# Side work of a three-part recurrent loop cut into small pieces and spread over its steps

## The reference, cut to what matters

```python
def lstm(prev_h, prev_c, xz_t):                 # L2 cond
    i, f, o, g = gates(xz_t + prev_h @ Wh)
    next_c = f * prev_c + i * g
    return o * tanh(next_c)

xp = silu(h @ W_in.T)                           # L2 attn, h from the LSTM
k, v, q, beta = ...                             # projections of xp, beta by a sigmoid
def step(S, inp):
    kn = k / (norm(k) + 1e-06)
    delta = v - einsum('bhij,bhj->bhi', S, kn)
    S = tanh(beta[..., None] * S + delta[..., None] * kn[..., None, :])
    Sq = einsum('bhij,bhj->bhi', S, q)
    return S, Sq * silu(Sq)
x = x + cell_out @ W_out.T

next_h = tanh(prev_h @ Wh + x_t @ Wx)           # L2 cond2, on the new x
```

## Time and profile before

| what | us |
|---|---|
| median of 3 runs | 3451.38 |
| lowest and highest | 3448.74, 3456.43 |
| the profiled execution | 3455.16 |
| its span, first to last instruction | 3453.4 |

### The profile page before, as it was taken

The page is one execution under the profiler, slowest core; times in us unless marked ns, Lnnn a source line. Parts: engine busy times, 40 slices in busy tenths (PEclk is TensorE's granted clock), DMA queues, the critical chain, the costliest instruction groups (busy, mean ns, idle before and its releaser), DMA issues. The chain is left out here.

```text
span 3453.4 us, 94785 instructions
## 1 busy us (share of the span) xinstructions
PE 2884.6 (84%) x35913; PEld 2169.6 (63%) x35915; DVE 1844.7 (53%) x7113; ACT 1151.5 (33%) x4428; POOL 761.3 (22%) x1477
## 2 busy tenths in 40 slices
PE   5889999956888894688899998987447799999988
PEld 3557888843556664456666666665314478888755
...
GB/s 75 2 2 0 0 0 0 0 33 1 2 2 0 1 0 64 96 76 65 87 85 64 86 87 63 79 95 59 37 0 1 2 0 0 0 0 0 0 0 12
DMA packets 106860, 101.37 MB, mean 29 GB/s; under 512 B 95616, under 2 KB 95616, under 8 KB 97536
## 3 DMA queue, kind: packets, MB, share of 16 engines
...
## 5 line engine op out<-in xcount | busy, mean ns | idle before, releaser
L578 POOL TENSOR_TENSOR l2r_beta_s<-l2r_state,l2r_beta_f 128x256 f32<-128x256 f32 x512 | 366.7, 737 | 547.0 <-ACT l2r_state L484 477.9
L484 ACT ACTIVATE l2r_state<-l2r_pre 128x256 f32<-128x256 f32 x512 | 190.5, 416 | 255.4 <-DVE l2r_pre L707 255.4
L381 PE MATMUL l2r_o_ps<-l2r_rows,l2r_outer 32*128 32x128 f32 x2048 | 207.0, 492 | 49.4 <-DVE l2r_rows L699 49.4
L707 DVE TENSOR_TENSOR l2r_pre<-l2r_o_ps,l2r_beta_s 128x256 f32<-128x256 f32 x512 | 193.5, 419 | 67.3 <-PE l2r_o_ps L381 66.2
L369 PE MATMUL l2r_d_ps<-l2r_state,l2r_kq 128*32 128x128 f32 x2056 | 206.3, 419 | 14.9 <-ACT l2r_state L484 13.4
L381 PEld LDWEIGHTS l2r_o_ps<-l2r_rows,l2r_outer 32*128 32x128 f32 x2048 | 139.2, 306 | 77.5 <-issue 70.5
L347 PEld LDWEIGHTS l2r_r_ps<-l2r_r_ring,main_even_layers 128*128 128x128 f32 x512 | 128.9, 312 | 92.4 <-issue 80.2
L699 DVE TENSOR_TENSOR l2r_rows<-l2r_d_ps,main_even_layers 128x128 f32<-128x128 f32 x257 | 74.5, 290 | 172.8 <-PE l2r_d_ps L369 162.0
L334 PEld LDWEIGHTS l2r_lstm_ps<-l2r_h_ring,l2r_w_part 128*128 128x128 bf16 x3072 | 103.5, 105 | 93.3 <-DVE l2r_h_low L693 53.7
L347 PE MATMUL l2r_r_ps<-l2r_r_ring,main_even_layers 128*128 128x8 f32 x512 | 149.3, 365 | 9.6 <-ACT l2r_r_ring L492 9.6
L133 PE MATMUL l3r_acc<-l3r_xw,main_base 128*128 x512 | 154.9, 389 | 1.6 <-issue 1.6
...
## 6 DMA issues: line engine op xcount, KB each, us to landing
l2r_beta_f<-l2r_beta_store SPq DMA_DIRECT2D x256, 256.0 KB, 7.0
...
l2r_beta_store<-l2r_beta_tok SPq DMA_DIRECT2D x256, 8.0 KB, 1.5
...
l2r_v_store<-l2r_v_part SPq DMA_DIRECT2D x128, 24.0 KB, 2.0
...
```

The source lines that it names most:

```text
L381: last = nc.tensor.matmul(o_ps[:, c, 0:P], outer[chunk_rows(c), n // TC % 2, n % TC, :, :].rearrange("p a b -> p (a b)"), rows[chunk_rows( ...
L484: nc.scalar.activation(state[:, h * 2 * P:(h + 1) * 2 * P], pre[:, h * 2 * P:(h + 1) * 2 * P], ACT.Tanh).then_inc(state_ready[h], 1)
L578: nc.gpsimd.tensor_tensor(beta_s[:, half], state[:, half], beta_f[:, q % BETA_SLOTS, n % QUARTER, half], ALU.mult).then_inc(s["bs_ready"], 1)
L707: nc.vector.tensor_tensor(pre[:, half].rearrange("p (c n) -> p c n", c=2), o_ps[:, 2 * h:2 * h + 2, 0:P], beta_s[:, half].rearrange("p (c ...
```

## The change

The LSTM's bank becomes two (`lstm_psa`, `lstm_psb`), each with the sums of eight LSTM steps and eight RNN steps; the inputs are written in halves, one gate of eight steps (64 columns) at a time, at steps given by `LSTM_PIECES`, and the RNN's inputs in three pieces of one, eight and seven steps. The token projections become six 128-column products at steps 2 to 7, q one product at each of steps 9 and 10, the transposes go to step 11. The square root becomes a guess by a shift and three Newton iterations, 14 operations of 128x8 on POOL at steps 6 to 8; DVE waits for them at step 8. The product for kn_tok goes from DVE to POOL, step 9; the squares go from POOL to ACT, step 10; POOL's k layouts are two each at steps 13 and 14. Stores of kn, v and beta are 2, 2 and 4 DMAs a wave; beta is stored first and v is loaded ahead of beta. In DRAM the step now lies inside the batch, so beta_f arrives in runs of 512 B (4 steps x 32 values) where a partition's run was 8,192 B. The amount of data is the same.

```diff
-        v_store = nc.dram_tensor(f"{tag}_v_store", (3 * HEADS2, 2, TC, BH, N2), BF16, kind="Internal").ap()
-        beta_store = nc.dram_tensor(f"{tag}_beta_store", (4, TC, 2, 2, BH, N2), F32, kind="Internal").ap()
+        v_store = nc.dram_tensor(f"{tag}_v_store", (3 * HEADS2, 2, BH, TC, N2), BF16, kind="Internal").ap()
+        beta_store = nc.dram_tensor(f"{tag}_beta_store", (4, 2, HG, BH, TC, N2), F32, kind="Internal").ap()
...
+        def lstm_at(n, first, last):
+            at = n % TCH * 4 * B
+            return lstm_ps[n % TC // TCH][:, at + first * B:at + last * B]
+        def rnn_at(n, count=1):
+            half, slot = (1, n % TC - 1) if 1 <= n % TC <= TCH else (0, (n - TCH - 1) % TC)
+            at = (4 * TCH + slot) * B
+            return lstm_ps[half][:, at:at + count * B]
...
+        LSTM_PIECES = {0: (0,), 3: (1,), 4: (2,), 5: (3,)}, {1: (0, 1), 2: (2,), 4: (3,)}
...
+                def rnn_inputs(w, lo, hi):
+                    if lo == 0:
+                        pe.wait_ge(s["x_added"], w + 1)
+                        pe.wait_ge(s["r_ready"], w * TC + 1)
+                    if lo == 1:
+                        pe.wait_ge(s["h_ready"], min((w + 4) * TC, T) + 1)
...
-                    if step in (2, 3):
+                    if 2 <= step < 8:
...
+                        if what >= 1:
+                            pe.wait_ge(s["kv_ready"], 2 * w + what)
+                        cols = HEADS2 * N2 // 2
+                        to, of = (what % 2 * 2 + part) * cols, (what * 2 + part) * cols
+                        last = nc.tensor.matmul(m_ps[:, to:to + cols], xp[:, :], w_tok[:, of:of + cols], start=True, stop=True)
+                        if part == 1:
+                            last.then_inc(s[("k_psum", "v_psum", "beta_psum")[what]], 1)
+                    if step in (9, 10):
+                        g = step - 9
+                        pe.wait_ge(s["beta_in"], w + 1)
+                        last = nc.tensor.matmul(m_ps[:, (2 + g) * CH:(3 + g) * CH], w_q[:, g * P:(g + 1) * P], xp[:, :],
+                                                start=True, stop=True)
+                        if g == 1:
+                            last.then_inc(s["q_psum"], 1)
...
-                        if rnn is not None and step >= 1:
+                        if rnn is not None:
+                            if step == 0:
+                                rnn_inputs(rnn, 0, 1)
                             rnn_product(rnn * TC + step)
                         if delta is not None:
                             spread_delta(n)
+                        if lstm is not None:
+                            if rnn is not None and step in (0, TCH):
+                                pe.wait_ge(s["r_ready"], rnn * TC + step + 2)
+                            lstm_products(lstm * TC + step)
+                        if step % TCH == 0 and has_bias(k, int(step == 0)):
+                            lstm_bias(*((k, 1) if step == 0 else (k + 1, 0)))
                         if rnn is not None and step == 0:
-                            rnn_inputs(rnn)
-                            rnn_product(rnn * TC)
+                            rnn_inputs(rnn, 1, TCH + 1)
+                        if rnn is not None and step == TCH:
+                            rnn_inputs(rnn, TCH + 1, TC)
                         if lstm is not None:
-                            if lstm >= 1 and step == 0:
-                                lstm_bias(lstm)
-                                for g in range(4):
-                                    lstm_inputs(lstm, g)
-                            lstm_products(lstm * TC + step)
+                            lstm_pieces(lstm, step, rnn)
...
-                    if step == 6:
-                        act.wait_ge(s["ssq_ready"], w + 1)
-                        nc.scalar.activation(norm[:, :], ssq[:, :], ACT.Sqrt).then_inc(s["norm_ready"], 1)
...
+                    if step >= 13:
+                        for g in ((0,), (1, 2), (3,))[step - 13]:
...
+                        nc.scalar.activation(sq_sq[:, :, :], sq[:, :, :], ACT.Square).then_inc(s["sq_sq_ready"], 1)
...
+                    pool.wait_ge(s["root_ready"], 14 * w + 4 * k + part + 2)
+                    if part == 0:
+                        last = nc.gpsimd.tensor_tensor(norm[:, :], ssq[:, :], root, ALU.mult)
+                    if part == 1:
+                        last = nc.gpsimd.tensor_tensor(norm[:, :], norm[:, :], root, ALU.mult)
+                    if part == 2:
+                        last = nc.gpsimd.tensor_scalar(norm[:, :], norm[:, :], -0.5, 1.5, ALU.mult, ALU.add)
+                    if part == 3:
+                        last = nc.gpsimd.tensor_tensor(root, root, norm[:, :], ALU.mult)
+                    last.then_inc(s["root_ready"], 1)
...
+                        pool.wait_ge(s["root_ready"], 14 * w + 1)
+                        nc.gpsimd.tensor_scalar(guess[:, :], guess[:, :], -1, 0x5F375A86, ALU.mult,
+                                                ALU.add).then_inc(s["root_ready"], 1)
+                        for part in range(4):
+                            root_part(w, 0, part)
+                    if step == 7:
+                        for part in range(4):
...
+                    if step == 9:
+                        pool.wait_ge(s["inv_ready"], 2 * (w + 1))
...
+                        nc.gpsimd.tensor_tensor(kn_tok[:, :, :], k_tok[:, :, :],
+                                                inv[:, :].unsqueeze(2).broadcast_to([P, HEADS2, N2]), ALU.mult).then_inc(s["kn_ready"], 1)
...
-                    if step in (12, 13, 14, 15):
+                    if step in (13, 14):
                         pool.wait_ge(s["knt_ready"], w + 1)
-                        g, h = divmod(step - 12, 2)
...
-                    if step == 2:
+                    if step == 1:
...
+                        dve.wait_ge(s["ssq_ready"], w + 1)
+                        nc.vector.tensor_scalar(guess[:, :], ssq[:, :].bitcast(I32), 1, None,
+                                                ALU.logical_shift_right).then_inc(s["root_ready"], 1)
+                    if step == 8:
...
+                        dve.wait_ge(s["beta_psum"], w + 1)
+                        if w >= 1:
+                            dve.wait_ge(s["beta_stored"], 16 * 4 * w)
+                        nc.vector.tensor_tensor(beta_tok[:, :], m_ps[:, 0:HEADS2 * N2], beta_bias, ALU.add).then_inc(s["beta_in"], 1)
...
-                        dve.wait_ge(s["inv_ready"], 2 * w + 2)
...
-                        nc.vector.tensor_tensor(kn_tok[:, :, :], k_tok[:, :, :],
-                                                inv[:, :].unsqueeze(2).broadcast_to([P, HEADS2, N2]), ALU.mult).then_inc(s["kn_ready"], 1)
...
-                    if step == 11:
...
-                    if step == 12:
...
+                        sp.dma_start(beta_f[chunk_rows(m), q % BETA_SLOTS, :, :, :].rearrange("p c t i -> p c (t i)"),
+                                     beta_store[m, :, :, :, part * QUARTER:(part + 1) * QUARTER, :].rearrange("h g b t i -> (h g b) (t i)")
+                                     .unsqueeze(0).broadcast_to([32, 2 * HG * BH, QUARTER * N2])).then_inc(beta_loaded[q % BETA_SLOTS], 16)
...
+                    for h in range(2):
                         for g in range(HG):
-                            sp.dma_start(beta_store.rearrange("m t h g b i -> g h b t m i")[g, h, n],
-                                         beta_tok[TC * b:TC * (b + 1), g * P:(g + 1) * P].rearrange("p (m i) -> p m i", i=N2)
+                            sp.dma_start(beta_store[:, h, g].rearrange("m b t i -> (b t) m i"),
+                                         beta_tok[BH * TC * h:BH * TC * (h + 1), g * P:(g + 1) * P].rearrange("p (m i) -> p m i", i=N2)
...
                     if proj is not None:
+                        store_beta(proj)
                         store_kn(proj)
                         load_kn(proj)
                         store_v(proj)
-                        store_beta(proj)
+                        load_v(proj)
                         load_beta(proj, 0)
-                        load_v(proj)
```

220 lines of the change are left out of this document (107 added, 113 removed).

## The result

The changed kernel takes **3345.9 us** (median of 4 runs, 3342.7 to 3348.9); the kernel before 3453.1 us (4 runs, 3448.7 to 3456.4). The ratio is 0.969, with a 95% interval of 0.9673 to 0.9707: 107 us or 3.1% less. 3351 us was forecast, with a range of 3325 to 3398. The profiled execution has a span of 3340.9 us beside 3453.4 before, 112.5 less.

The account below looks back on a forecast made before the run. PE was taken as nearly full, steps bound by the delta chain or PE's work. Gains of 68 (waves), 12 (start), 13 (waves 0 and 1) and 8 (last steps), less 0.5, made 100.5 us: 3351 us, range 3325 to 3398.

Parts of the forecast that it names:

- The step law: Layer 2 loop: a step lasts the larger of the 3.25 us delta-state chain and PE's 2.64 us plus side work.
- The 0.5 us for handovers: Added to the 59.2 us wave for handovers between engines that the packed picture leaves out, giving 59.7 us.
- the 1 us added to waves 0 and 1: Handover allowance on the first two waves, forecast at 55.4 and 58.4 us; their gain was put at 13 us.
- The cut pieces: PE side work: some 14 halved products a wave, 64 columns each, priced at 0.50 us apiece.
- the rival with the lone price: Each cut piece on PE costs the 0.73 us of a product standing alone; 3391 us, chance 0.08.
- the lower bound: A 64-column piece on PE costs only its share of the columns, 0.24 us, giving a wave of 56.5 us.
- Both waits: From step 15 to 0, PE's 3.03 us wait for v and POOL's 4.13 us for beta go, 4 us in hand.
- the one-step RNN input: PE side work from step 15 to 0, priced at 0.35 us beside the output pair; period 4.03 us.
- The root: Steps 6 to 8: 14 POOL operations at 0.28 us finish at 8.6 us, before DVE at 10.4 us, so hidden.
- The table loads: ACT loses three loads of 1,283 ns a wave, blocked 3.9 us; gain already inside the 65.4 us wave.
- The packets: Beta loads in 512 B packets take 0.04 to 0.06 us each; a quarter takes 5 to 8 us and hides.
- the rival's threshold of 0.117 us: Packet time at which beta loads start to bind; the slow-beta case took 0.14 us, 3541 us, chance 0.05.

Follow-up runs that it names:

- the gap: Changed kernel with LSTM input and output products moved between retrieve and spread on PE: 3352.9 us, wave 59.61 us.
- transfers alone: Kernel before with only the new beta and v layouts, fewer stores and v loaded ahead of beta: 3403.7 us, ratio 0.9852.

## Why the prediction was right, point by point

- **The step law held.** The larger of 3.25 us and 2.64 us plus side work gave 59.2 us for a wave; it is 59.3. Waves 0 and 1, forecast with 55.4 and 58.4, took 55.3 and 58.3. Fourteen of 16 periods are within 0.08 us of the forecast. The two misses are steps 0 and 8 (+0.13, +0.25), both with half a bias and RNN inputs: the bias is 1735.57 - 1735.25 = 0.32 us where 0.27 was taken, and all pieces together 1.48 and 1.37 us where 1.42 and 1.27 were. That explains 0.06 and 0.10; the rest is open. It also foretold what four edits do to a wave, to within 0.05 us for three of them and 0.5 for the gap.
- **The 0.5 us for handovers was wrong.** With the 1 us added to waves 0 and 1 it makes 7 us, nearly all of the 7.3 by which the gain from the loop's begin on (107.8) exceeds the 100.5 forecast. The law was read from whole steps, so the handovers were in it already.
- **The cut pieces** of 64 columns cost 0.47 us in a row, where 0.50 was taken, and a lone product of 128 columns 0.67 (1736.73 - 1736.06), where 0.65 was. So the rival with the lone price for every piece is out, and so is the lower bound: half the columns bring nothing here.
- **The turn.** Both waits are gone as forecast. What the prediction didn't see is the third one behind them, ACT's RNN tanh ahead of the state tanh. The forecast gave the right sum by luck, because it priced the one-step RNN input from the order without asking what that piece is for; a change without it would have been forecast too fast, as transfers alone were.
- **The root** was hidden, and its operations took 0.28 us. Its slack was mis-sized: 1.8 us was worked out, but POOL's chain took 1704.31 - 1695.08 = 9.2 us in place of 8.6 and DVE came after 9.8 in place of 10.4, so 0.56 is left. The sum ran the beta products right behind one another's side work; each waits for its step's state instead, 0.52 and 0.72 us in these rows. Against that, the text left out the 1.04 us of idle time behind DVE's wait. Longer operations would have used up all four: (0.52 + 0.72 + 0.56 + 1.04) / 14 + 0.28 = 0.48 us each is my estimate of the threshold, where 0.41 was forecast. The two runs with a longer root tested only the last two of the four.
- **The table loads** were named but not priced on their own ("not counted again"). They are the largest part of a wave's gain. A forecast by parts would have had to say 2.7 us; the one by step periods didn't need it.
- **The packets** took 0.027 to 0.046 us, where 0.04 to 0.06 was taken, and the rival's threshold of 0.117 us was far. The Trainium skill (DMA: Bandwidth & Descriptors, Specifications) asks for 512 B at least; the same 98.1 MB take 14.4% of the engines' span with loads in 512 B packets and 13.7% with 256 B, so no run shows an edge at 512 B.
- **Start, ends and clock.** From the loop's begin to the first state tanh it is 12.3 us (12 forecast), waves 0 and 1 14.3 (13), the last 31 steps 8.1 (8; 31 x 3.25 is 100.8 and not the 101.3 of the text, and one period at 3.66 makes 101.2), the clock 0.50. The sign "no step over 4.5" held but for the one period of 4.91. That the profiled loop began 4.7 us earlier was no part of any term.
